# A graph network block on one core: first ffn layer as three-pass split products, convolution bias added by POOL, new step orders

## The chip, the cores and the metric

The kernel runs on one core of one Trainium2 chip. The core has TensorE (PE, matrix products), VectorE (DVE), ScalarE (ACT), GpSimd (POOL) and SyncE (SP, which here issues every DMA). Each engine runs its own list of instructions in order, and the engines wait for each other by semaphores only. The metric is device time in microseconds (us), the median of the runs; one more execution was profiled.

## The reference, cut to what matters

`x` is 16 batches of 512 nodes with 256 features, `adj` one 512 x 512 graph for all of them. Everything is float32. Two layers follow each other, each with a norm and a relu ahead of it and a residual behind it:

```python
h = relu(layernorm(x))
h = elu(gat_heads(h, adj, W_heads, a_heads))     # 4 heads, softmax over 512 neighbours
out = elu(gat_heads(h, adj, W_out[None], a_out)) # one more head ("back"), input width 4 * 256
ffn = relu(out @ w1 + b1) @ w2 + b2
x = x + layernorm(ffn + out) * gamma + beta
h = relu(layernorm(x))                           # second layer, a graph convolution
deg = a.sum(axis=1)                              # a = adj as float
x = x + deg[None, :, None] * (h @ Wi.T + b) + einsum('ij,bjo->bio', a, h @ Wj.T)
```

The change touches `out @ w1` and the term `deg * b`.

## The kernel before

A batch lies as 4 tiles of 128 nodes. The work of a batch is cut into named steps, and every engine has a written list of words `step:which@batch`. `FIRST` and `LAST` are lists of their own for the start and the end (in `LAST` batches are counted from the end, so -1 is the last one), and `ROUND` is run for t = 8 to 15, where `@k` stands for batch t - k. Batches overlap in this way: while the heads of one batch run, the ffn of the one before and the convolution of the one before that are under way. A step has a part on several engines, each under the same name in the list of its engine; nothing reorders the lists at run time.

The steps of one batch, in the order of the data:

- `load`, `norm_in`, `norm_in_out` (statistics on DVE, the power of -0.5 on POOL, scale and relu on ACT), `turn_in` (PE transposes; ACT copies the high part and DVE subtracts it to get the low part).
- `m1:hp`, the product with the weights of head h for half p of the nodes; `f2turn`, `f2send`, `f2bcast`: one column of scores is transposed, sent to HBM and broadcast to all partitions by SP.
- for ten units (five heads, two halves; units 4 and 5 are the back head): `rowmax`, `rowmath` (DVE), `args` (ACT), `rinv`, `scale` (DVE), `turn_p` (8 transposes on PE), `probs` (ACT high part, DVE low part), `attend` (24 matmuls), `elu_neg`, `elu_exp` (ACT), `elu_out` (DVE), `hx` (ACT), `hx_lo` (POOL).
- `mix2` (24 matmuls for each of 4 tiles), then the back head's units.
- `turn_out` (8 transposes of `out` and one ACT copy to `ff[:, 0]`, float32), `ffn1` (float32 products with `w1`, relu on ACT), `ffn2` (float32), `add_b2`, `norm_ff`, `gamma`, `x_beta`, `x2`.
- `norm_gc`, `norm_gc_out`, `turn_gc`, `conv_in:0` and `conv_in:1` (products of both halves of `W_gc`; DVE adds `deg` times the left half to `xb`), `conv` (32 matmuls with the transposed graph), `store`.

Most products are split: both operands are held as an f32r high part and an f32r low part, and `product` sums high x high, low x high and high x low, three matmuls in place of one float32 product. The float32 products are `ffn1`, `ffn2` and all transposes; a float32 product shows as two records in the trace. In `conv_in` the bias enters through a fourth kind of matmul: `pick` has ones in two rows, `brow` holds the bias as a high and a low row, and `also=` places that one matmul of 256 columns behind the first one of each tile, four for each batch.

PSUM is four pairs of banks. Every PE step takes the pair that has been in use longest (`take` waits until it was read, `lend` says by whom), so a step can start only when the step four places ahead of it in PE's list has been read out.

## Time and profile before

| | before |
|---|---|
| median of 3 runs | 1393.72 us (1392.29 to 1399.7) |
| profiled execution, its own time | 1393.09 us |
| span from the first to the last instruction | 1391.3 us |
| mean granted TensorE clock | 0.984 |
| busy share: PE, PE weight load, DVE, ACT, POOL | 95%, 89%, 79%, 80%, 25% |
| DMA, mean | 40 GB/s |

All durations below come from the profiled execution. Its own time is its span plus 1.8 us around it. A busy share counts the time in which at least one instruction of the engine runs. Matmuls are pipelined: a matmul of 256 columns lasts 0.28 us in its record while the next one starts 0.12 us later, so what a matmul takes from the engine is read from the distance of starts, not from the duration.

### The profile page before, as it was taken

The numbers are of one execution on the slowest core, as the hardware profiler recorded it, in microseconds if no ns is written. First come the engines' busy times: TensorE is split into PE (matmuls) and PEld (weight loads), VectorE is DVE, ScalarE is ACT, GpSimd is POOL, SyncE is SP. The second block draws the span as 40 slices with busy tenths as digits, with TensorE's granted clock in tenths as the row PEclk, the third lists the DMA queues.
The fourth block names the chain that finished last, engine by engine and source line by source line (L and its number), as shares of the span: only waits on it lengthen the run. The fifth ranks groups of instructions, "written<-read, shape, count | busy, mean of one in ns | idle before, by whom it ended". The sixth has DMA issues, their size and how long they took to land.

```text
span 1391.3 us, 27533 instructions
## 1 busy us (share of the span) xinstructions
PE 1317.3 (95%) x10024; PEld 1243.7 (89%) x10024; DVE 1101.2 (79%) x2859; ACT 1113.2 (80%) x2143; POOL 341.1 (25%) x234
## 2 busy tenths in 40 slices
PE   3799999999999999999999999999999999999884
PEld 3799999999999999999999999999999989999763
DVE  7798878897888888788888878888787878878442
ACT  4789988888888888888888888888788878878531
POOL 0021222314132131413213141231414132131411
PEclk9799999999999999999999999999999999999997
DMA  6101011011111101111110111110111020011000
GB/s 211 62 24 54 17 32 47 25 38 32 39 46 32 46 24 33 37 39 47 31 47 18 30 46 39 47 31 17 43 43 39 24 61 17 17 39 39 24 31 16
DMA packets 42742, 55.15 MB, mean 40 GB/s; under 512 B 2864, under 2 KB 30832, under 8 KB 42480
## 3 DMA queue, kind: packets, MB, share of 16 engines
q1 hardware_dynamic: 42608, 53.39, 12.6%
q8 instruction: 81, 1.33, 0.4%
q14 instruction: 53, 0.43, 0.1%
HBM read 44.83 MB, written 8.55 MB: 38 GB/s over the span
## 4 chain that ended last, share of the span: by engine, by line
PE 85%; DVE 5%; ACT 4%; DMA 3%; issue 2%; POOL 0%; SPq 0%; POOLq 0%; ACTq 0%
PE ps L1007 60%; PE ps L1077 9%; PE ps L1177 5%; PE ps L1141 4%; PE ps L1129 4%; DMA f_rows<-f2row 2%; PE ps L1150 1%; PE ps L1039 1%; PE ps L1115 1%; DVE arg L898 1%; ACT arg L700 1%; PE ps L1068 1%; PE ps L1010 1%; DVE prob_lo L875 1%; ACT prob_hi L706 0%
## 5 line engine op out<-in xcount | busy, mean ns | idle before, releaser
L598 POOL TENSOR_TENSOR hx_lo<-elu,hx_hi 128x512 fp32r<-128x512 f32 x128 | 168.0, 1314 | 827.6 <-ACT hx_hi L730 827.6
L1007 PE MATMUL ps<-prob_hi,whx_hi 128*128 128x256 f32 x1024 | 297.9, 291 | 3.0 <-DVE prob_lo L875 2.8
L1007 PE MATMUL ps<-prob_hi,whx_lo 128*128 128x256 f32 x1024 | 289.2, 282 | 0.0
L1007 PE MATMUL ps<-prob_lo,whx_hi 128*128 128x256 f32 x1024 | 289.1, 282 | 0.0
L898 DVE CUSTOM_DVE_ANT_0 arg<-f2bc,mask 128x512 f32<-128x512 f32 x320 | 233.6, 767 | 11.8 <-DMA f2bc<-f_rows 10.5
L700 ACT ACTIVATE arg<-arg,nmax 128x512 f32<-128x512 f32 x320 | 227.1, 713 | 1.9 <-DVE nmax L909 1.8
L875 DVE TENSOR_TENSOR prob_lo<-ps,prob_hi 128x1024 fp32r<-128x1024 f32 x160 | 195.1, 1220 | 37.8 <-ACT prob_hi L706 37.2
L696 ACT ACTIVATE arg<-arg,fcol 128x512 f32<-128x512 f32 x320 | 212.4, 714 | 7.5 <-DVE gmax L898 7.5
L1007 PEld LDWEIGHTS ps<-prob_hi,whx_hi 128*128 128x128 f32 x1024 | 195.3, 191 | 6.0 <-DVE prob_lo L875 4.0
L1007 PEld LDWEIGHTS ps<-prob_hi,whx_lo 128*128 128x128 f32 x1024 | 195.7, 191 | 0.6 <-issue 0.5
L1007 PEld LDWEIGHTS ps<-prob_lo,whx_hi 128*128 128x128 f32 x1024 | 195.5, 191 | 0.0
L706 ACT ACTIVATE prob_hi<-ps 128x1024 fp32r<-128x1024 f32 x160 | 162.2, 1015 | 27.9 <-PE ps L1077 27.1
L1077 PE MATMUL ps<-ident,arg 128*128 128x128 f32 x1280 | 167.8, 275 | 7.1 <-DVE arg L924 6.5
L1077 PEld LDWEIGHTS ps<-ident,arg 128*128 128x128 f32 x1280 | 146.2, 142 | 17.7 <-DVE arg L924 7.3
L1007 PE MATMUL ps<-wh_hi,hT_hi 128*128 128x258 f32 x512 | 152.5, 298 | 6.2 <-DVE hT_lo L875 5.8
L1007 PE MATMUL ps<-wo_hi,hx_hi 128*128 128x258 f32 x512 | 146.4, 286 | 0.2 <-POOL hx_lo L598 0.2
L1007 PE MATMUL ps<-wh_lo,hT_hi 128*128 128x258 f32 x512 | 146.2, 286 | 0.0
L924 DVE TENSOR_SCALAR arg<-arg,rinv 128x512 f32<-128x512 f32 x320 | 144.0, 493 | 2.7
L1007 PE MATMUL ps<-wh_hi,hT_lo 128*128 128x258 f32 x512 | 145.7, 285 | 0.0
L1007 PE MATMUL ps<-wo_lo,hx_hi 128*128 128x258 f32 x512 | 144.7, 283 | 0.0
L1007 PE MATMUL ps<-wo_hi,hx_lo 128*128 128x258 f32 x512 | 144.4, 282 | 0.0
L935 DVE SCALAR_TENSOR_TENSOR elu<-elu,ps 128x512 f32<-128x512 f32 x128 | 87.7, 685 | 67.3 <-ACT elu L725 66.0
(131 smaller groups left out, 3144.1 us busy)
## 6 DMA issues: line engine op xcount, KB each, us to landing
f2bc<-f_rows SPq DMA_DIRECT2D x80, 256.0 KB, 3.3
xin<-in_x SPq DMA_DIRECT2D x16, 512.0 KB, 4.1
xb<-in_x SPq DMA_DIRECT2D x16, 512.0 KB, 3.9
out_x<-xb SPq DMA_DIRECT2D x16, 512.0 KB, 2.9
f_rows<-f2row SPq DMA_DIRECT2D x80, 2.0 KB
ff<-in_L_gnn_a_heads SPq DMA_DIRECT2D x1, 1024.0 KB, 7.9
arg<-in_adj SPq DMA_DIRECT2D x1, 1024.0 KB, 10.0
ff<-in_L_gnn_W_out SPq DMA_DIRECT2D x1, 1024.0 KB, 5.6
```

The costliest lines, as they stand in the source:

```text
L598: pool.tensor_tensor(out=hx[1][:, 2 * c.h:2 * c.h + 2, c.u * HN:(c.u + 1) * HN], in0=elu[:, c.buf, :, :], in1=hx[0][:, 2 * c.h:2 * c.h + 2 ...
L696: act.activation(a[:, n, :], a[:, n, :], ACT.Prelu, bias=f1[:, n:n + 1], alpha=SLOPE).then_inc(arg_lin, 1)
L700: i = act.activation(a[:, n, :], a[:, n, :], ACT.Exp, bias=nmax[:, c.abuf, n:n + 1], accum_out=rsum[:, c.abuf, n:n + 1])
L706: act.activation(prob[0][:, c.buf, :, :].rearrange("p j i -> p (j i)"), pairs[c.pair][:, :, :].rearrange("p a n -> p (a n)"), ACT.Copy).th ...
L875: return dve.tensor_tensor(out=dst, in0=src, in1=hi.bitcast(fp32), op=ALU.subtract)
L898: dve.tensor_tensor_reduce(out=arg[:, c.abuf, n, :], in0=f2bc[:, head % F2S, :], in1=mask[:, 2 * c.u + n, :], scale=1.0, scalar=-3.0e38, o ...
L924: i = dve.tensor_scalar(arg[:, c.abuf, n, :], arg[:, c.abuf, n, :], rinv[:, c.abuf, n:n + 1], None, ALU.mult)
L935: dve.scalar_tensor_tensor(out=dst, in0=elu[:, c.buf, :, :], scalar=-1.0, in1=pairs[c.pair][:, :, 0:F], op0=ALU.add, op1=ALU.max).then_inc ...
L1007: i = pe.matmul(out, a, b_, start=(k == 0), stop=(k == n - 1))
L1077: i = pe.transpose(p[:, j, n, :], arg[:, c.abuf, n, j * P:(j + 1) * P], ident[:, :])
L1129: i = pe.matmul(pairs[c.pair][:, o, :], w1_sb[:, k, o * P:(o + 1) * P], outT[:, k, :], start=(k == 0), stop=(k == KC - 1))
L1177: i = pe.matmul(pairs[c.pair][:, n // 2, (n % 2) * F:(n % 2 + 1) * F], adjT[:, j, n * P:(n + 1) * P], mj, start=(j == 0 and s == 0), stop= ...
```

## The change

Three things change.

1. `w1` is held as f32r high and low parts (`w1_prep` on ACT, `w1_low` on DVE, once), `turn_out` gets a high part by ACT and a low part by DVE, both in `h2T` in place of `ff[:, 0]`, and `ffn1` becomes 12 f32r matmuls of 512 columns by `product`. ACT's `turn_out` waits for `conv` of the batch before, since that one reads `h2T`. `w1` is staged in the second slot of `f2bc`, so the first broadcast to that slot waits for `w1_low`.
2. The matmuls with `pick` and `brow` go, and with them what prepared them. Once, DVE computes `deg_b` (degree times bias, 4 instructions, `degb`), and POOL adds it to `xb` in each batch (`bias`), behind `norm_gc_out` and ahead of DVE's accumulation in `conv_in`.
3. All lists of all engines are new. Apart from the new steps (`w1_prep`, `w1_low`, `degb`, `bias`, DVE's `turn_out`) and `brow`, which goes, they hold the same steps in another order.

```diff
@@ -7,239 +7,239 @@
     "SP": """
-    load@0 load@1 load_wo@0 f2send:0@0 f2bcast:0@0 f2send:1@0 load_adj@0 f2bcast:1@0 load@2 f2send:2@0 f2bcast:2@0 f2send:3@0
...
+    load@0 load@1 f2send:0@0 load_wo@0 f2bcast:0@0 f2send:1@0 f2bcast:1@0 f2send:2@0 f2send:3@0 f2bcast:2@0 f2bcast:3@0
...
     "PE": """
-    turn_in@0 gc_turn@0 m1:00@0 m1:01@0 m1:10@0 f2turn:0@0 m1:11@0 f2turn:1@0 m1:20@0 m1:21@0 m1:30@0 m1:31@0 turn_p:0@0
-    f2turn:2@0 adj_turn:0@0 adj_turn:1@0 turn_p:1@0 turn_in@1 attend:0@0 attend:1@0 f2turn:3@0 turn_p:2@0 m1:00@1 turn_p:3@0
...
+    turn_in@0 m1:00@0 m1:01@0 m1:10@0 m1:11@0 f2turn:0@0 gc_turn@0 m1:20@0 m1:21@0 m1:30@0 f2turn:1@0 f2turn:2@0 m1:31@0
+    turn_p:0@0 f2turn:3@0 turn_p:1@0 turn_in@1 attend:0@0 attend:1@0 m1:00@1 turn_p:2@0 turn_p:3@0 attend:2@0 m1:01@1
+    adj_turn:0@0 turn_p:6@0 attend:3@0 f2turn:0@1 m1:10@1 m1:11@1 turn_p:7@0 attend:6@0 adj_turn:1@0 f2turn:1@1 attend:7@0
...
     "ACT": """
-    wh_prep:0@0 wh_prep:1@0 wh_prep:2@0 norm_in_out@0 wh_prep:3@0 mask:0@0 gc_turn@0 turn_in@0 m1:00@0 m1:01@0 mask:1@0
-    m1:10@0 wo_prep:0@0 f2turn:0@0 m1:11@0 m1:20@0 m1:21@0 f2turn:1@0 m1:30@0 norm_in_out@1 m1:31@0 args:0@0 args:1@0
...
+    wh_prep:0@0 wh_prep:1@0 norm_in_out@0 turn_in@0 w1_prep@0 m1:00@0 wh_prep:2@0 wh_prep:3@0 mask:0@0 m1:01@0 m1:10@0 m1:11@0
+    f2turn:0@0 gc_turn@0 m1:20@0 mask:1@0 m1:21@0 m1:30@0 f2turn:1@0 wo_prep:0@0 args:0@0 args:1@0 norm_in_out@1 m1:31@0
...
     "DVE": """
-    norm_in@0 norm_in_out@0 wh_low:0@0 wh_low:1@0 wh_low:2@0 wh_prep:0@0 wh_prep:1@0 wh_prep:2@0 mask:0@0 wh_low:3@0
-    wh_prep:3@0 mask_end:0@0 turn_in@0 mask:1@0 norm_in@1 gc_turn@0 m1:00@0 mask_end:1@0 norm_in_out@1 m1:01@0 m1:10@0
-    wo_prep:0@0 wo_prep:1@0 m1:11@0 wo_prep:2@0 wo_prep:3@0 wo_prep:4@0 wo_prep:5@0 rowmax:0@0 wo_prep:6@0 wo_prep:7@0
-    rowmath:0@0 rowmax:1@0 rowmath:1@0 rinv:0@0 m1:20@0 scale:0@0 m1:21@0 m1:30@0 rowmax:2@0 m1:31@0 rinv:1@0 rowmath:2@0
...
+    norm_in@0 norm_in_out@0 wh_low:0@0 wh_low:1@0 wh_prep:0@0 wh_prep:1@0 turn_in@0 mask:0@0 wh_prep:2@0 wh_low:2@0 m1:00@0
+    wh_prep:3@0 m1:01@0 m1:10@0 wh_low:3@0 mask_end:0@0 m1:11@0 mask:1@0 m1:20@0 gc_turn@0 mask_end:1@0 norm_in@1 rowmax:0@0
+    rowmath:0@0 w1_low@0 m1:21@0 rowmax:1@0 rowmath:1@0 wo_prep:0@0 norm_in_out@1 wo_prep:1@0 rowmax:2@0 rinv:0@0 wo_prep:2@0
+    m1:30@0 scale:0@0 rowmath:2@0 rinv:1@0 wo_prep:3@0 m1:31@0 scale:1@0 probs:0@0 rowmax:3@0 wo_prep:4@0 wo_prep:5@0
...
 ROUND = {
...
     "PE": """
-    m1:31@5 turn_in@4 attend:1@5 f2turn:2@5 turn_p:2@5 m1:00@4 turn_gc@7 m1:01@4 turn_p:3@5 attend:2@5 conv_in:0@7 f2turn:3@5
-    conv_in:1@7 turn_p:4@6 attend:3@5 m1:10@4 turn_p:5@6 attend:4@6 f2turn:0@4 turn_p:6@5 attend:5@6 conv@7 m1:11@4 turn_p:7@5
-    turn_out@6 attend:6@5 ffn1@6 turn_p:8@5 attend:7@5 m1:20@4 turn_p:9@5 f2turn:1@4 attend:8@5 m1:21@4 ffn2@6 m1:30@4
-    attend:9@5 turn_p:0@4 mix2:0@5 mix2:1@5 turn_p:1@4 mix2:2@5 mix2:3@5 attend:0@4 f2turn:-1@5
+    f2turn:2@5 turn_p:2@5 m1:00@4 turn_gc@7 turn_p:3@5 m1:01@4 attend:2@5 conv_in:0@7 f2turn:3@5 conv_in:1@7 turn_p:4@6
+    attend:3@5 m1:10@4 turn_p:5@6 attend:4@6 turn_p:6@5 f2turn:0@4 attend:5@6 m1:11@4 conv@7 turn_out@6 attend:6@5 turn_p:7@5
+    turn_p:8@5 ffn1@6 f2turn:1@4 attend:7@5 attend:8@5 turn_p:9@5 m1:20@4 m1:21@4 ffn2@6 m1:30@4 attend:9@5 mix2:0@5
+    turn_p:0@4 mix2:1@5 turn_p:1@4 mix2:2@5 mix2:3@5 attend:0@4 f2turn:-1@5 m1:31@4 turn_in@3 attend:1@4
...
     "ACT": """
...
+    elu_neg:3@6 elu_exp:3@6 m1:10@5 hx:2@6 probs:5@7 hx:3@6 elu_neg:4@7 elu_exp:4@7 probs:6@6 args:7@6 elu_neg:5@7 elu_exp:5@7
+    f2turn:0@5 m1:11@5 args:8@6 turn_out@7 elu_neg:6@6 elu_exp:6@6 probs:7@6 hx:6@6 probs:8@6 args:9@6 ffn1@7 elu_neg:7@6
...
     "DVE": """
...
+    norm_in@5 elu_out:4@8 probs:6@7 rowmax:8@7 rinv:7@7 rowmath:8@7 elu_out:5@8 m1:11@6 scale:7@7 norm_in_out@5 conv@9
+    rowmax:9@7 rinv:8@7 scale:8@7 turn_out@8 elu_out:6@7 probs:7@7 rowmath:9@7 probs:8@7 rowmax:0@6 rinv:9@7 rowmath:0@6
...
+    norm_ff@8 m1:30@6 elu_out:9@7 rinv:1@6 scale:1@6 norm_ff_out@8 rowmath:2@6 rowmax:3@6 probs:0@6 mix2:0@7 probs:1@6 x2@8
+    rowmath:3@6 rinv:2@6 norm_gc@8 mix2:1@7 scale:2@6 rinv:3@6 norm_gc_out@8 elu_out:0@6 scale:3@6 m1:31@6 turn_in@5
+    elu_out:1@6 probs:2@6 m1:00@5 turn_gc@8 rowmax:4@7
...
     "POOL": """
-    hx_lo:0@5 hx_lo:1@5 hx_lo:2@5 hx_lo:3@5 norm_in@3 hx_lo:6@5 add_b2@6 hx_lo:7@5 hx_lo:8@5 x_beta@6 norm_ff@6 hx_lo:9@5
-    gamma@6 norm_gc@6
+    hx_lo:0@5 bias@7 hx_lo:1@5 hx_lo:2@5 hx_lo:3@5 norm_in@3 hx_lo:6@5 hx_lo:7@5 add_b2@6 hx_lo:8@5 x_beta@6 norm_ff@6
+    hx_lo:9@5 gamma@6 norm_gc@6
...
 LAST = {
...
     "PE": """
...
-    attend:8@-1 turn_p:9@-1 ffn2@-2 attend:9@-1 mix2:0@-1 mix2:1@-1 mix2:2@-1 mix2:3@-1 f2turn:-1@-1 turn_gc@-2 conv_in:0@-2
-    turn_p:4@-1 conv_in:1@-2 turn_p:5@-1 attend:4@-1 attend:5@-1 conv@-2 turn_out@-1 ffn1@-1 ffn2@-1 turn_gc@-1 conv_in:0@-1
-    conv_in:1@-1 conv@-1
...
+    attend:8@-1 attend:9@-1 mix2:0@-1 mix2:1@-1 mix2:2@-1 mix2:3@-1 turn_gc@-2 f2turn:-1@-1 conv_in:0@-2 conv_in:1@-2 conv@-2
+    turn_p:4@-1 turn_p:5@-1 attend:4@-1 attend:5@-1 turn_out@-1 ffn1@-1 ffn2@-1 turn_gc@-1 conv_in:0@-1 conv_in:1@-1 conv@-1
...
@@ -278,18 +278,16 @@
...
-        w1_sb = sb("w1_sb", [P, KC, F])
+        w1x = [sb(f"w1_{s}", [P, KC, F], f32r) for s in ("hi", "lo")]
@@ -330,12 +328,14 @@
...
+        w1_st = f2bc[:, 1, :].rearrange("p (k o) -> p k o", k=KC)
...
+        deg_b = ff[:, 0, :, :]
@@ -343,6 +343,7 @@
...
+        outT = [t[:, :, :].rearrange("p c f -> p (c f)").rearrange("p (k n) -> p k n", k=KC) for t in h2T]
@@ -522,7 +526,7 @@
...
-            sp.dma_start(w1_sb[:, :, :], w1.rearrange("(k p) o -> p k o", p=P)).then_inc(ld[LD_W1], 16)
+            sp.dma_start(w1_st, w1.rearrange("(k p) o -> p k o", p=P)).then_inc(ld[LD_W1], 16)
@@ -546,6 +550,8 @@
...
+                if head == 1:
+                    sp.wait_ge(s_w1, 1)
...
             def load_back(c):
@@ -559,7 +565,6 @@
...
             def load_wo(c):
...
-                sp.wait_ge(s_pick, 1)
@@ -579,14 +584,9 @@
         def _(pool):
...
-            pool.memset(pick_st, 0.0).then_inc(s_zeroed, 1)
-            pool.wait_ge(s_zeroed, 3)
+            pool.wait_ge(s_zeroed, 2)
...
-            for z in range(2):
-                pool.affine_select(out=pick_st, in_=pick_st, compare_op=ALU.not_equal, fill=1.0, base=-z,
-                                   pattern=[[0, P]], channel_multiplier=1).then_inc(s_const, 1)
-                pool.wait_ge(s_const, 2 + z)
@@ -619,7 +619,13 @@
...
+            def bias(c):
+                if c.b == 0:
+                    pool.wait_ge(s_bias, 1)
+                pool.wait_ge(ln_out["gc"], c.b + 1)
+                pool.tensor_tensor(out=xb[:, :, :], in0=xb[:, :, :], in1=deg_b, op=ALU.add).then_inc(bias_added, 1)
@@ -638,6 +644,10 @@
             def wo_prep(c):
...
+            def w1_prep(c):
+                act.wait_ge(ld[LD_W1], 16)
+                act.activation(w1x[0][:, :, :], w1_st, ACT.Copy).then_inc(s_w1_hi, 1)
@@ -730,22 +740,19 @@
...
             def mix2(c):
-                if c.b == 0:
-                    act.wait_ge(s_brow, 1)
...
             def turn_out(c):
+                act.wait_ge(o_turned, c.b + 1)
+                wait(act, conv_done, c.b)
+                act.activation(outT[0], pairs[c.pair][:, :, :], ACT.Copy).then_inc(oT_ready, 1)
...
+            def ffn1(c):
...
-                act.wait_ge(o_turned, c.b + 1)
-                act.activation(ff[:, 0, :, :], pairs[c.pair][:, :, :].rearrange("p a n -> p (a n)").rearrange("p (k n) -> p k n", k=NC),
-                               ACT.Copy).then_inc(oT_ready, 1)
...
-            def ffn1(c):
-                if c.b == 0:
@@ -817,23 +824,23 @@
...
-                if c.info == 0:
-                    dve.wait_ge(s_const, 3)
-                    dve.tensor_copy(pick[:, :], pick_st).then_inc(s_pick, 1)
...
             def gc_turn(c):
...
-            def brow_(c):
+            def w1_low(c):
+                dve.wait_ge(s_w1_hi, 1)
+                dve.tensor_tensor(out=w1x[1][:, :, :], in0=w1_st, in1=w1x[0][:, :, :].bitcast(fp32), op=ALU.subtract).then_inc(s_w1, 1)
...
+            def degb(c):
...
-                part, hi = wk[:, 3, :], w2x[:, 0, :]
-                link(dve.tensor_copy(hi, b_g))
-                link(dve.tensor_tensor(out=part, in0=b_g, in1=hi.bitcast(fp32), op=ALU.subtract))
-                link(dve.tensor_scalar(part, part, ident[:, 1:2], None, ALU.mult))
-                link(dve.scalar_tensor_tensor(out=part, in0=hi.bitcast(fp32), scalar=ident[:, 0:1], in1=part, op0=ALU.mult, op1=ALU.add))
-                dve.tensor_copy(brow[:, :], part).then_inc(s_brow, 1)
+                dve.wait_ge(s_adj, 1)
+                dve.wait_ge(s_adj_turned, 2)
+                for n in range(NC):
+                    i = dve.tensor_scalar(deg_b[:, n, :], b_g, deg[:, n:n + 1], None, ALU.mult)
+                i.then_inc(s_bias, 1)
@@ -928,7 +935,7 @@
...
-                        dve.wait_ge(s_brow, 1)
+                        dve.wait_ge(s_bias, 1)
@@ -940,6 +947,10 @@
...
+            def turn_out(c):
+                dve.wait_ge(oT_ready, c.b + 1)
+                lo(outT[1], pairs[c.pair][:, :, :], outT[0]).then_inc(oT_lo, 1)
@@ -962,7 +973,7 @@
...
-                dve.wait_ge(ln_out["gc"], c.b + 1)
+                dve.wait_ge(bias_added, c.b + 1)
@@ -998,7 +1009,7 @@
...
-            def product(out, terms, also=None):
+            def product(out, terms):
@@ -1006,8 +1017,6 @@
...
-                        if also and k == 1:
-                            pe.matmul(*also, start=False, stop=False)
...
             def gc_turn(c):
@@ -1114,20 +1123,19 @@
...
-                lend((c.pair,), (oT_ready, c.b + 1))
...
-            outT = ff[:, 0, :, :].rearrange("p c f -> p (c f)").rearrange("p (k n) -> p k n", k=KC)
+                lend((c.pair,), (oT_lo, c.b + 1))
...
             def ffn1(c):
...
-                    pe.wait_ge(ld[LD_W1], 16)
-                pe.wait_ge(oT_ready, c.b + 1)
+                    pe.wait_ge(s_w1, 1)
+                pe.wait_ge(oT_lo, c.b + 1)
...
-                    for k in range(KC):
-                        i = pe.matmul(pairs[c.pair][:, o, :], w1_sb[:, k, o * P:(o + 1) * P], outT[:, k, :], start=(k == 0), stop=(k == KC - 1))
-                    i.then_inc(f1_done, 1)
+                    part = slice(o * P, (o + 1) * P)
+                    product(pairs[c.pair][:, o, :],
+                            [(w1x[0][:, k, part], w1x[1][:, k, part], outT[0][:, k, :], outT[1][:, k, :]) for k in range(KC)]).then_inc(f1_done, 1)
...
             def ffn2(c):
@@ -1155,14 +1163,12 @@
             def conv_in_(c):
...
-                    pe.wait_ge(s_brow, 1)
...
-                                [(h2T[0][:, n, k * P:(k + 1) * P], h2T[1][:, n, k * P:(k + 1) * P], wg[0][:, k, :], wg[1][:, k, :]) for k in range(KC)],
-                                also=(pairs[c.pair][:, i, 0:F], pick[:, :], brow[:, :]))
+                                [(h2T[0][:, n, k * P:(k + 1) * P], h2T[1][:, n, k * P:(k + 1) * P], wg[0][:, k, :], wg[1][:, k, :]) for k in range(KC)])
...
```

## Rows read from the trace of the kernel before

**Rows 1.** Page, part 1: busy us, share of span, instructions.

```profile
PE 1317.3 (95%) x10024; PEld 1243.7 (89%) x10024; DVE 1101.2 (79%) x2859; ACT 1113.2 (80%) x2143; POOL 341.1 (25%) x234
```

**Rows 2.** Windows: busy us (instructions) by engine, granted clock, DMA share, GB/s.

```profile
0.00:40.00 40.00, 17.24 (x95) 15.88 (x96) 30.91 (x132) 15.36 (x31) 3.47 (x12) 0.96 0.56 184
...
40.00:80.00 40.00, 29.15 (x212) 27.98 (x211) 32.84 (x98) 34.90 (x75) 2.75 (x2) 0.83 0.22 67
...
400.00:800.00 400.00, 398.08 (x3087) 379.02 (x3086) 335.15 (x844) 336.06 (x647) 106.90 (x70) 1.00 0.12 34
...
1300.00:1340.00 40.00, 33.59 (x238) 31.06 (x238) 20.91 (x56) 19.05 (x36) 7.01 (x5) 0.91 0.02 7
...
1340.00:1391.30 51.30, 25.07 (x117) 19.25 (x116) 13.98 (x33) 8.77 (x14) 9.06 (x5) 0.80 0.10 31
```

**Rows 3.** Groups by line, TensorE: count, busy us, mean ns, idle.

```profile
L1129 PE MATMUL ps<-ff,w_sb 128*128 128x512 f32 x128 | 57.7, 594 | 1.2 <-ACT ff L744 1.1
...
L1010 PE MATMUL ps<-brow,pick 128*128 128x256 f32 x64 | 18.5, 289 | 0.0
```

**Rows 4.** Timeline of TensorE, conv_in of one batch: start, duration, line.

```profile
693.12 0.28 PE L1010 MATMUL ps<-brow,pick 128*128 128x256 f32 x1
...
693.23 0.40 PE L1007 MATMUL ps<-wg_hi,h2T_lo 128*128 128x512 f32 x1
...
694.40 0.39 PE L1007 MATMUL ps<-wg_hi,h2T_hi 128*128 128x512 f32 x1
```

**Rows 5.** Timeline of TensorE: turn_out, ffn1 and what follows.

```profile
718.32 1.04 PE L1115 MATMUL ps<-ident,wk 128*128 128x128 f32 x8
...
722.06 3.59 PE L1129 MATMUL ps<-ff,w_sb 128*128 128x512 f32 x8
...
725.49 1.04 PE L1077 MATMUL ps<-ident,arg 128*128 128x128 f32 x8
...
726.28 0.36 PE L1007 MATMUL ps<-prob_hi,whx_hi 128*128 128x256 f32 x1
...
726.49 0.28 PE L1007 MATMUL ps<-prob_hi,whx_lo 128*128 128x256 f32 x1
```

**Rows 6.** Groups by line of DVE and POOL.

```profile
L875 DVE TENSOR_TENSOR h2T_lo<-ps,h2T_hi 128x1024 fp32r<-128x1024 f32 x16 | 19.6, 1223 | 11.8 <-ACT h2T_hi L758 11.8
...
L834 DVE TENSOR_SCALAR wk<-wk,ident 128x256 f32<-128x256 f32 x1 | 0.4, 353 | 0.0
...
L605 POOL TENSOR_TENSOR wk<-wk,b_bc 128x1024 f32<-128x1024 f32 x16 | 38.4, 2403 | 45.4 <-PE ps L1115 45.4
```

**Rows 7.** Timelines of POOL and DVE: gamma beside a rowmax.

```profile
749.21 2.86 POOL L619 TENSOR_TENSOR wk<-wk,gamma_bc 128x1024 f32<-128x1024 f32 x1 [0.67 <-ACT wk L667]
...
749.75 2.87 DVE L898 CUSTOM_DVE_ANT_0 arg<-f2bc,mask 128x512 f32<-128x512 f32 x1
```

**Rows 8.** Timelines of ACT and DVE: norm_gc_out, conv_in.

```profile
679.90 2.06 ACT L667 ACTIVATE ff<-xb,shift_gc,rstd_gc 128x256 f32<-128x256 f32 x4
...
698.27 0.87 DVE L968 SCALAR_TENSOR_TENSOR xb<-ps,deg,xb 128x256 f32<-128x256 f32 x2
```

**Rows 9.** Timelines of ACT, DVE, TensorE: the first 50 us.

```profile
9.54 2.06 ACT L667 ACTIVATE xin<-xin,shift_in,rstd_in 128x256 f32<-128x256 f32 x4
...
19.50 1.01 ACT L675 ACTIVATE hT_hi<-ps 128x1024 fp32r<-128x1024 f32 x1
...
20.76 1.22 DVE L875 TENSOR_TENSOR hT_lo<-ps,hT_hi 128x1024 fp32r<-128x1024 f32 x1
...
48.50 1.97 PE L1077 MATMUL ps<-ident,arg 128*128 128x128 f32 x8 [6.00 <-DVE arg L924]
```

**Rows 10.** Chain that ended last: the last 80 us.

```profile
1314.35 0.61 ACT w2x_hi L738
...
1321.71 0.68 DVE arg L898
...
1342.03 0.89 PE ps L1115 x8
```

More of the change, by code:

```diff
@@ L67 @@
+    probs:0@1 rowmax:3@1 rinv:2@1 mix2:0@0 scale:2@1 rowmath:3@1 degb@0 rinv:3@1 m1:31@1 norm_in_out@2 scale:3@1 probs:1@1
+    elu_out:0@1 mix2:1@0 probs:2@1 turn_in@2 elu_out:1@1 m1:00@2 rowmax:4@0
     """,
@@ L180 @@
[L180 to L183 removed]
+    f2turn:-1@-7 m1:31@-6 hx:0@-6 turn_in@-5 norm_gc_out@-8 elu_neg:1@-6 elu_exp:1@-6 probs:2@-6 f2turn:2@-6 m1:00@-5
```

368 lines of the change are left out of this document (179 added, 189 removed).

## The prediction

> **What bounds the kernel now.** I read the page first for the busy shares, then the windows, to see where each engine has room, then the groups of TensorE and its timeline for what a matmul takes, and last the waits and the chain at both ends. TensorE is busy 95% of the span, the next engines 80% and 79% [rows 1]. The windows say where the missing 5% lies. From 400 to 800 us TensorE is busy 398.08 of 400 us at full clock, while DVE and ACT are busy 335 and 336 us and POOL 107 [rows 2]. In the first 80 us it is busy 46.4 us (17.24 + 29.15), and in the last 51.3 us only 25.07, there at a mean granted clock of 0.80 [rows 2]. So the kernel has three parts: a start and an end in which chains through several engines decide, and between them some 1220 us in which the time is the sum of what TensorE issues. A microsecond taken from TensorE's list in the middle is worth one microsecond, as long as the others keep up.
>
> **ffn1.** Before, one ffn1 is 8 records of 512 columns, from 722.06 to the next step's start at 725.49: 3.43 us [rows 5]. The new one is 12 f32r matmuls of 512 columns. The same form runs in conv_in: five starts from 693.23 to 694.40, 0.234 us each [rows 4]. 12 x 0.234 = 2.81 us, a gain of 0.62 us for a batch, 9.9 us for 16. One bound is that nothing comes of it in batches where ffn1 then waits for its operand; the other is 10 us.
>
> **The bias matmuls.** There are 64 [rows 3], and the one at 693.12 is followed at 693.23 [rows 4], so one takes 0.11 us; other matmuls of 256 columns are up to 0.12 apart. 64 x 0.115 = 7.4 us (7.0 to 7.7).
>
> **Changes of type.** The first f32r matmul after float32 transposes takes 726.49 - 726.28 = 0.21 us, 0.09 more than its neighbours [rows 5]. Counting such places in TensorE's lists gives 226 before and 229 after, with ffn1 counted on its new side: +0.3 us. Sum for TensorE: 9.9 + 7.4 - 0.3 = 17.0 us less.
>
> **What the others get.** DVE gets 16 subtractions of 1024 columns at 1.22 us [rows 6], 19.6 us, and loses only the single preparation of the bias rows; w1_low (one subtraction of 512 columns, about half of that) and degb (4 x 0.35 us [rows 6]) come once. DVE goes from 79% to about 82%, still below TensorE. ACT's turn_out stays one copy of 1024 columns, 1.01 us as in turn_in [rows 9], and w1_prep comes once. POOL gets 16 additions of 2.40 us [rows 6], 38 us on an engine that is idle for three quarters of the span. The cover of the new low part is the work between turn_out and ffn1. Before, that was one attend, from about 719.1 (718.32 and 0.8 us of transposes) to 722.06, 2.9 us [rows 5]. In the new round it is attend:6, turn_p:7 and turn_p:8, 2.9 + 2 x 0.79 = 4.5 us (one turn_p is 725.49 to 726.28 [rows 5]). Needed are 1.01 + 1.22 = 2.2 us, so some 2.2 us are left for a queue on ACT or DVE. If the cover went, each batch would pay up to these 2.2 us. Behind ACT's turn_out stand elu_neg:6 and probs:7, and attend:7 waits for the latter. Its new wait for conv of the batch before costs nothing: conv stands directly ahead of turn_out in TensorE's list. The bias step starts when norm_gc_out ends, at 681.96 in the batch of [rows 8], and DVE's accumulation comes at 698.27: 16 us for 2.4 us of work. In the last batch turn_gc, its two copies and conv_in (12 x 0.234 x 2 = 5.6 us) lie in between, about 9 us, so it is hidden there too. Behind bias on POOL stand hx_lo:1 to hx_lo:3; a late norm_gc_out would delay them, then elu_neg:3 on ACT, which waits for the buffer. For waits that the new lists bring to the middle I add 2 us. Its idle share is 1.92 of 400 us [rows 2], 0.5%, which is 6 us over 1220: if all of it went, the term would be -6, and if it became three times as much, +12.
>
> **The start.** Before, ACT's turn_in runs at 19.50, 8 us after norm_in_out ended at 11.60, because the mask step and gc_turn stand ahead of it, and the first product waits for its low part until 21.98 [rows 9]. In the new lists nothing but the transposes (2.0 us at the low clock, as for those at 48.50 [rows 9]) stands between: 11.6 + 2.0 + 1.0 + 1.2 = 15.8, some 6 us earlier. w1_prep is put ahead of ACT's m1:00, where it must wait for the load of w1; m1:00 on TensorE runs meanwhile. Next late is the first turn_p, at 48.50 for want of scale:0. On DVE three wo_prep steps stand ahead of scale:0 in place of eight, but f2bcast:0 now stands behind load_wo on SP, whose wait for the prepared weights and whose 1 MB come first, and f2bcast:1 waits for w1_low. adj_turn, at the low clock before, moves behind the first attends. DVE is busy 30.9 of the first 40 us [rows 2], so I do not take the whole 6 us: 4 us gained, between 8 gained and 3 lost.
>
> **The end.** From the last mix2 (1314.35) to turn_out of the last batch (1342.03) the chain takes 27.7 us [rows 10]; the conv of the batch before, 32 matmuls of 256 columns x 0.12 = 3.8 us, stands in it directly ahead of turn_out. In the new list this conv stands ahead of turn_p:4, in the time in which the last softmax is on its way (its rowmax starts 7.4 us after mix2 [rows 10]). Against these 3.8 us go the low part of turn_out, 1.2 us, and that ACT's args:4 and DVE's rowmath:4 now stand behind conv_in:1, about 1 us. I take 1.5 us gained, between 4 gained and 3 lost.
>
> **The sum.** -17.0 - 4 - 1.5 + 2 = -20.5 us. On the profiled execution's 1393.09 us that is 1372.6. The median of the runs lies 0.6 us above that execution, so 1373.
>
> **The shared port.** A POOL step can hold DVE up: the rowmax that starts at 749.75, 0.54 us into POOL's gamma, takes 2.87 us and ends with it [rows 7], where another takes 0.68 [rows 10]. The Trainium skill, SBUF — State Buffer, section Who interferes with whom, says that a DVE instruction with two SBUF inputs, or a tensor_scalar in a two-port mode, and a GpSimd instruction that reads SBUF exclude each other, and the later one is blocked for the whole instruction; by that rule the trace agrees. By the same rule the bias step would lock out a rowmax or a scale sixteen more times, and if each met one and all of it reached TensorE, the sum would be 15 us longer than before instead of 20 shorter.
>
> **Rivals.**
>
> *The middle gives back part.* The lists are rigid, and a late copy or a buffer still in use in each batch costs TensorE half a microsecond: 16 x 0.5 = 8 us on top of the sum, 1381. For it: DVE gets 19.6 us, and ACT and DVE are at 84% of the middle [rows 2]. Against: the margin of 2.2 us at the one new chain. Chance 0.2.
>
> *The ends lose.* load_wo ahead of the broadcast delays the first softmax, and the last one is delayed by conv_in:1: no gain at the end and 1 us lost at the start, 5.5 + 1 us on top, 1379.5. Chance 0.1.
>
> *Slower: bias blocks DVE.* Each bias locks out one rowmax or scale for up to 2.87 - 0.68 = 2.2 us, and what hangs on it is late on TensorE: 16 x 2.2 = 35 us on top, 1408. It decides (0.5% slower) from (20.5 + 7) / 16 = 1.7 us for a batch. For it: [rows 7]. Against: in the new round DVE runs elu_out:1, probs:2, m1:00 and turn_gc while bias is due, each with an operand in PSUM, and rowmax:4 only behind them; and DVE has 16% of the middle to catch up. Chance 0.05.
>
> *Nothing comes of it.* TensorE's busy share only hides that another chain sets the pace, and its shorter work turns into waiting: 1392. Against: 398 of 400 us busy, and starts that follow each other at the pipeline's distance. Chance 0.05.
>
> **How the numbers follow.** My forecast has 0.6, with 1366 to 1379 as its own range. The range goes down to 1365, a little below start and end both at their good bounds (1373 - 4 - 2.5 = 1366.5), and up through the first two rivals to 1385, where the middle's term is at its bound of +12. That leaves out the last two rivals and some margin, 2 in 10. A measurement here tells about 0.5%, 7 us, from no change. Faster by that: the forecast and the first two rivals, 0.9; within it: the fourth, 0.05; slower: the third, 0.05.
>
> **What would show it.** ffn1 as 12 starts 0.23 us apart and no L1010 group; TensorE still busy above 99% from 400 to 800 us, with a distance between equal steps of successive batches about 1.1 us shorter; ffn1 without idle time ahead of it; DVE's added group of 16 at 1.22 us; first product near 16 us and first turn_p before 48.5; DVE's rowmax and scale no longer on average. The prediction is wrong if TensorE's idle time in the middle comes to more than 18 us, or if the start or the end moves by more than its bounds.

## The result, and the profile of the changed kernel

The changed kernel takes 1377.67 us, the median of 4 runs (1376.74 to 1378.36); the kernel before has 1396.71 in 4 runs (1392.29 to 1400.56). The ratio is 0.9876, with a 95% interval of 0.9849 to 0.9903: 1.2% faster. 1373 was forecast with a range of 1365 to 1385. The profiled executions differ by 14.7 us (1393.09 and 1378.36; spans 1391.3 and 1376.6), where the sum forecast 20.5. That is 4 us less than the medians tell, because all runs of the kernel before lie in two groups, 1391.1 to 1394.4 and 1396.1 to 1400.6 us, and the profiled one is of the faster group; what sets the two apart is not shown.

The page, part 1, answers to [rows 1].

```profile
span 1376.6 us, 27572 instructions
...
PE 1299.2 (94%) x10024; PEld 1248.1 (91%) x10024; DVE 1100.5 (80%) x2874; ACT 1113.1 (81%) x2144; POOL 370.1 (27%) x247
```

TensorE is busy 18.1 us less and idle 77.4 us instead of 74.0: -18.1 + 3.4 = -14.7. The windows, columns as in [rows 2], say where the idle time is.

```profile
0.00:80.00 80.00, 48.41 (x318) 45.20 (x319) 66.23 (x237) 52.95 (x108) 5.32 (x11) 0.87 0.40 129
80.00:160.00 80.00, 74.58 (x612) 72.28 (x611) 64.02 (x173) 71.94 (x143) 15.39 (x12) 1.00 0.11 28
240.00:1200.00 960.00, 959.86 (x7545) 929.23 (x7544) 808.82 (x2068) 827.72 (x1594) 278.55 (x181) 1.00 0.12 38
1200.00:1290.00 90.00, 84.45 (x645) 80.36 (x644) 63.57 (x159) 67.89 (x129) 31.03 (x20) 1.00 0.08 22
```

The same windows of the kernel before:

```profile
0.00:80.00 80.00, 46.39 (x304) 43.87 (x305) 63.75 (x229) 50.26 (x105) 6.22 (x14) 0.89 0.39 125
80.00:160.00 80.00, 77.58 (x624) 73.73 (x623) 69.25 (x181) 74.18 (x145) 18.03 (x13) 1.00 0.11 31
240.00:1200.00 960.00, 955.51 (x7385) 907.26 (x7384) 796.27 (x2020) 812.52 (x1563) 252.46 (x166) 1.00 0.12 36
1200.00:1290.00 90.00, 89.13 (x676) 82.94 (x675) 70.09 (x173) 74.33 (x142) 20.18 (x13) 1.00 0.12 39
```

At the start the new kernel gets 2.0 us ahead in the first 80 us and gives 3.0 back in the next 80. In the middle its idle time falls from 4.49 us of 960 to 0.14. From 1200 to 1290 us TensorE is idle 5.55 us where it was idle 0.87. The new kernel is 20 us ahead there; over the same work of the kernel before, from 1220 to 1311.6 us, the idle time is 0.87 us as well.

A clean measure of the middle is the distance between POOL's gamma steps of successive batches (timeline of POOL; start, duration): first before, then after.

```profile
505.07 2.86 POOL L619 TENSOR_TENSOR wk<-wk,gamma_bc 128x1024 f32<-128x1024 f32 x1 [0.68 <-ACT wk L667]
586.41 2.86 POOL L619 TENSOR_TENSOR wk<-wk,gamma_bc 128x1024 f32<-128x1024 f32 x1 [0.67 <-ACT wk L667]
```

```profile
501.11 2.41 POOL L619 TENSOR_TENSOR wk<-wk,gamma_bc 128x1024 f32<-128x1024 f32 x1 [0.62 <-ACT wk L677]
580.50 2.41 POOL L619 TENSOR_TENSOR wk<-wk,gamma_bc 128x1024 f32<-128x1024 f32 x1 [0.63 <-ACT wk L677]
```

A batch takes 79.39 us instead of 81.34, 1.95 less. Forecast were 1.1. Gamma itself is 0.45 us shorter; in [rows 7] it ran beside a rowmax, and here no rowmax starts while it runs.

ffn1 is now three groups of 64 matmuls (TensorE's groups; busy us, mean ns, idle before), to be held against L1129 in [rows 3]. No group is left for brow and pick.

```profile
L1018 PE MATMUL ps<-h2T_hi,w_hi 128*128 128x512 f32 x64 | 27.3, 427 | 2.4 <-DVE h2T_lo L882 2.4
L1018 PE MATMUL ps<-h2T_hi,w_lo 128*128 128x512 f32 x64 | 26.4, 413 | 0.0
L1018 PE MATMUL ps<-h2T_lo,w_hi 128*128 128x512 f32 x64 | 26.1, 408 | 0.0
```

ffn1 waits 2.4 us in all, and that is the last batch alone. In the middle it waits for nothing (outT's parts lie in the h2T buffers and bear their name), but by little. Timelines of TensorE, ACT and DVE around one ffn1:

```profile
706.14 1.03 PE L1124 MATMUL ps<-ident,wk 128*128 128x128 f32 x8
706.93 0.36 PE L1018 MATMUL ps<-prob_hi,whx_hi 128*128 128x256 f32 x1
...
711.55 0.48 PE L1018 MATMUL ps<-h2T_hi,w_hi 128*128 128x512 f32 x1
```

```profile
707.21 1.03 ACT L751 ACTIVATE h2T_hi<-ps 128x1024 fp32r<-128x1024 f32 x1 [0.65 <-PE ps L1124]
```

```profile
708.89 0.89 DVE L931 TENSOR_SCALAR arg<-arg,rinv 128x512 f32<-128x512 f32 x2
709.69 1.22 DVE L882 TENSOR_TENSOR h2T_lo<-ps,h2T_hi 128x1024 fp32r<-128x1024 f32 x1
```

The high part is there at 708.24, but DVE still has rowmax:9, rinv:8 and scale:8 ahead of the low part, which starts at 709.69 and is ready at 710.91. Counted from the attend at 706.93, it takes 3.98 us, and the cover is 4.62. The margin is 0.64 us.

The end, timeline of TensorE (in square brackets the idle time before, and what ended it):

```profile
1323.23 1.97 PE L1124 MATMUL ps<-ident,wk 128*128 128x128 f32 x8 [2.07 <-DVE wk L942]
1327.58 0.80 PE L1018 MATMUL ps<-h2T_hi,w_hi 128*128 128x512 f32 x1 [2.37 <-DVE h2T_lo L882]
...
1328.60 0.63 PE L1018 MATMUL ps<-h2T_lo,w_hi 128*128 128x512 f32 x1
1329.02 0.63 PE L1018 MATMUL ps<-h2T_hi,w_hi 128*128 128x512 f32 x1
```

turn_out takes 1.97 us where it took about 1.04, and ffn1's matmuls start 0.42 us apart and not 0.23. The granted clock is 0.53 from 1323.23 to 1333.84, nearly all of it at the lower of the two levels (1.2 GHz); before the change it was 1.00 over the same steps (1342.03 to 1347.70).

### The profile page after: what moved, and what is told of

It reads as the page before. It is cut to its first block, busy times and chain, and to the rows that moved or that the text cites. A ratio compares the mean times of both kernels' runs of the same rounds, so it can differ in the third digit from the quotient of the medians.

```text
span 1376.6 us, 27572 instructions
## 1 busy us (share of the span) xinstructions
PE 1299.2 (94%) x10024; PEld 1248.1 (91%) x10024; DVE 1100.5 (80%) x2874; ACT 1113.1 (81%) x2144; POOL 370.1 (27%) x247
## 4 chain that ended last, share of the span: by engine, by line
PE 86%; ACT 5%; DVE 5%; issue 2%; DMA 1%; POOL 0%; SPq 0%; ACTq 0%; DVEq 0%
PE ps L1018 66%; PE ps L1086 9%; PE ps L1183 4%; PE ps L1149 4%; PE ps L1124 1%; PE ps L1158 1%; PE ps L1048 1%; ACT arg L710 1%; DVE arg L905 1%; DVE prob_lo L882 1%; ACT prob_hi L716 1%; PE ps L1077 1%; ACT arg L706 1%; ACT elu L731 1%; DMA f2bc<-f_rows 0%
## 5 line engine op out<-in xcount | busy, mean ns | idle before, releaser
L905 DVE CUSTOM_DVE_ANT_0 arg<-f2bc,mask 128x512 f32<-128x512 f32 x320 | 220.9, 728 | 4.3 <-PE ps L1086 2.9
L931 DVE TENSOR_SCALAR arg<-arg,rinv 128x512 f32<-128x512 f32 x320 | 147.0, 502 | 1.4
L731 ACT ACTIVATE elu<-ps 128x512 f32<-128x512 f32 x160 | 93.9, 587 | 64.6 <-PE ps L1018 62.2
```

What stands on the lines that cost most here:

```text
L731: act.activation(elu[:, c.buf, :, :], pairs[c.pair][:, :, 0:F], ACT.Relu, scale=-1.0).then_inc(elu_neg, 1)
L905: dve.tensor_tensor_reduce(out=arg[:, c.abuf, n, :], in0=f2bc[:, head % F2S, :], in1=mask[:, 2 * c.u + n, :], scale=1.0, scalar=-3.0e38, o ...
L931: i = dve.tensor_scalar(arg[:, c.abuf, n, :], arg[:, c.abuf, n, :], rinv[:, c.abuf, n:n + 1], None, ALU.mult)
```

## The experiments

Ratios are to runs of the kernel before on the same chip. The experiments ran on three chips, whose kernels before have medians of 1397.35 (e1 to e4), 1396.55 (e5 to e8) and 1394.03 us (e9 to e12), so medians of different groups can differ by up to 3 us for that alone. A batch is the mean of two distances between gamma steps, from about 430 to 590 us, and does not hang on this.

| run | median us | ratio to before, 95% interval | a batch, us |
|---|---|---|---|
| before | 1396.7 | 1 | 81.34 |
| changed kernel | 1377.67 | 0.9876 (0.9849 to 0.9903) | 79.40 |
| e1 both changes, old orders | 1412.79 | 1.0111 (1.0088 to 1.0133) | 81.8 |
| e2 new orders alone | 1392.56 | 0.9972 (0.9958 to 0.9986) | 80.50 |
| e3 ffn1 alone, old orders | 1415.57 | 1.0134 (1.0113 to 1.0156) | 82.0 |
| e4 bias alone, old orders | 1394.19 | 0.9982 (0.9965 to 0.9999) | 80.8 |
| e5 e1, ffn1 behind attend:7 | 1442.68 | 1.0344 (1.0321 to 1.0366) | 82.7 |
| e6 changed, conv behind attend:5 | 1379.84 | 0.9887 (0.9869 to 0.9905) | 79.4 |
| e7 changed, m1:21 first | 1375.17 | 0.9851 (0.9829 to 0.9873) | 79.4 |
| e8 changed, bias twice | 1388.62 | 0.9948 (0.9930 to 0.9966) | 80.10 |
| e9 e5, low part behind probs:7 | 1448.32 | 1.0383 (1.0358 to 1.0407) | 82.2 |
| e10 ffn1 alone, new orders | 1384.15 | 0.9929 (0.9908 to 0.9951) | 79.86 |
| e11 bias alone, new orders | 1386.14 | 0.9937 (0.9917 to 0.9958) | 80.05 |
| e12 e7 and a new last batch | 1389.13 | 0.9961 (0.9946 to 0.9976) | 79.4 |

**e1.** The new code in the lists of before, with the new steps put in.

```diff
 DVE ROUND
-    ... probs:7@5 ...
+    ... turn_out@6 probs:7@5 ...
 POOL ROUND
-    ... hx_lo:0@5 hx_lo:1@5 ...
+    ... hx_lo:0@5 bias@7 hx_lo:1@5 ...
 PE ROUND (as before)
     turn_p:7@5 turn_out@6 attend:6@5 ffn1@6 turn_p:8@5 attend:7@5
```

> Both code changes (first layer in three f32r passes, bias on POOL), but the steps of every engine in the orders of the kernel before; the new steps are put in by hand: DVE's turn_out ahead of probs:7, POOL's bias behind hx_lo:0 of two batches on, the preparations of the start behind m1. Theory A (the gain is TensorE's work, the orders only make room for it): the middle keeps nearly all of the 17 us of removed work, less about 1 us for each turn_out that has only attend:6 behind it; the start stays that of before, the end too. Median about 1382, 1379 to 1387. Rival B (the code alone gains nothing, the new orders are what makes it faster): 1391 to 1397, with ffn1 waiting for oT_lo over 1 us in each batch. Rival C (the new orders cost more at the start and the end than they give in the middle): under 1377.

1.1% slower than before, outside the range of all three; B's sign is there, a wait of ffn1 of over 1 us. TensorE's timeline and its group of ffn1 name the place:

```profile
644.80 1.04 PE L1126 MATMUL ps<-ident,wk 128*128 128x128 f32 x8
649.78 0.50 PE L1020 MATMUL ps<-h2T_hi,w_hi 128*128 128x512 f32 x1 [1.09 <-DVE h2T_lo L884]
```

```profile
L1020 PE MATMUL ps<-h2T_hi,w_hi 128*128 128x512 f32 x64 | 28.0, 438 | 23.0 <-DVE h2T_lo L884 22.8 <-DVE prob_lo L884 0.2
```

With attend:6 alone as cover, ffn1 waits for the low part in every batch, 22.8 us in all, more than the 17 us of removed work. The chain takes as long as in the changed kernel: the low part is ready at 649.73, 4.1 us behind the attend at 645.59. Here the queue is on ACT, though: its high part starts only at 647.25, behind args. TensorE is busy 8.7 us less than before and idle 25.5 us more (1308.6 of a span of 1408.1), so ffn1's waits are nearly all of the added idle time. That the busy time falls by 8.7 and not by 17 is in part the clock (mean granted 0.979, before 0.984) and the start of each wait, which counts as busy (see e2); the rest is open.

**e2.** The code of before in the new lists.

```diff
 DVE FIRST
-    ... probs:1@0 ...
+    ... probs:1@0 brow@0 ...
 (no turn_out, w1_prep, w1_low, degb, bias; all else as in the change)
```

> The code of the kernel before (fp32 first layer, bias as a matmul) in the new orders of every engine, with the steps that this code lacks left out and brow behind probs:1 of the first batch on DVE. Theory A (orders make room, work makes the gain): within 4 us of the kernel before, 1391 to 1400; the period of a batch stays between 80.5 and 81.5 us. Rival B (orders are the gain): 1378 to 1386. Rival C (the orders lose at both ends): 1400 to 1408, with the loss in the last four batches.

Faster by 0.3%. The median is what A expects, the batch is not: it is 0.84 us shorter, 1.0%, without any change of the work. Some 0.45% of it is idle time (4.49 us of the 960 from 240 to 1200 us before, 0.12 in e2). The rest counts as busy, but most of it is waiting too. TensorE's timeline of the kernel before, ahead of turn_gc and ahead of conv:

```profile
523.51 0.28 PE L1007 MATMUL ps<-wh_lo,hT_hi 128*128 128x258 f32 x1
524.00 1.06 PE L1150 MATMUL ps<-ident,ff 128*128 128x128 f32 x8 [0.21 <-DVE elu L935]
...
548.91 0.28 PE L1007 MATMUL ps<-w2x_lo,prob_hi 128*128 128x256 f32 x1
549.30 0.36 PE L1177 MATMUL ps<-h2T_hi,adjT 128*128 128x256 f32 x1
```

turn_gc starts 0.49 us behind the matmul ahead of it, in e2 0.16; conv 0.39, in e2 0.12. Together that is 0.6 of the 0.84 us. Only 0.3 of it shows as idle time, because the record of a matmul lasts 0.28 us where the next could start after 0.12: the first 0.16 us of a wait lie under it. So the old orders had two short waits in each batch, and the new ones have none. At the ends it is lost again: the profiled span is 1391.6 us, 0.3 more than before; of the gain only the 0.3% between the medians is left.

**e3 and e4.** One code change each in the old lists.

```diff
 e3: product(pairs[c.pair][:, i, :], [...],
+        also=(pairs[c.pair][:, i, 0:F], h2T[0][:, n, 0:P], wg[0][:, 0, 0:F]))
 e4: ffn1
+    i = pe.matmul(pairs[c.pair][:, o, :], w1x[0][:, k, part].bitcast(fp32), outT[0][:, k, :].bitcast(fp32), ...)
```

> The first layer in three f32r passes alone, in the orders of before. The bias stays on TensorE as a matmul of the same shape as before, but its operands are other tiles at hand (a piece of h2T and a row of wg), so the bias added is not that of the reference; POOL adds none. By the prediction's terms the work falls by 9.9 us and rises by 0.3: median 1384 to 1390 if the terms add up in the old orders, with 12 records in a group of ffn1 0.234 us apart. Rival (ffn1 waits for DVE's low part, which comes 2.2 us after turn_out while attend:6 covers 2.0): each batch gives back 0.3 us or more, 1389 to 1394.

> The bias on POOL alone, in the orders of before; the first layer stays at fp32 rate with four matmuls (it reads the rounded high parts only, so its result lacks the low parts; their number, shape and type of pass are those of before). By the prediction's terms 64 matmuls of 0.116 us go, 7.4 us: median 1385 to 1390. Rival (POOL's addition blocks the port it shares with DVE for about 2 us a batch and DVE is late for it): 1392 to 1400, with rowmax means over 780 ns.

e3 is 1.3% slower, worse than its rival, which had priced the missing cover at 0.2 us; its three-pass ffn1 waits just as in e1. e4 gains 0.5 us a batch, as the 0.46 of its matmuls, but its median is 0.2% under before, not 0.5%, and lies in the range of its rival. The rival's sign came too, a mean of 789 ns for rowmax (767 before), but not its cause in the middle: from 500 to 600 us the only long rowmax are those beside gamma, 2.88 us as before. What takes the gain back outside the middle is open. So what makes e1 slow in the middle is ffn1's operand alone.

**e5 and e9.** Both try to mend e1 by moving steps.

```diff
 e5, PE ROUND
-    turn_out@6 attend:6@5 ffn1@6 turn_p:8@5 attend:7@5
+    turn_out@6 attend:6@5 turn_p:8@5 attend:7@5 ffn1@6
 e9, also DVE ROUND
-    turn_out@6 probs:7@5
+    probs:7@5 turn_out@6
```

> Experiment e1 with one step moved: in TensorE's lists ffn1 stands behind attend:7 instead of behind attend:6, so that turn_p:8 and attend:7 (4 us) run while ACT and DVE make the high and low part of outT; ACT's and DVE's lists are those of e1. Theory A2 (e1 lost only by the wait of ffn1 for oT_lo, 1.7 us in each of 16 batches): about 27 us less than e1 less what the first batch loses because ffn2 stands directly behind: 1385 to 1392, no wait for h2T_lo over 0.5 us in the middle, period 80.2 to 80.8 us. Rival D (DVE's and ACT's queues in the old orders are what is late, whichever step shows it): the waits come back in front of other steps, median over 1400.

> Experiment e5 with one more step moved: DVE makes the low part of outT behind probs:7 instead of ahead of it, so that attend:7, which e5 put ahead of ffn1, no longer waits for it. Theory A3 (what the old orders lose is where DVE's new step of 1.2 us stands against probs:7 and ffn1, nothing else): the wait of 1.3 us in front of attend:7 goes, ffn1 starts 6 us behind turn_out with its operand ready, and the period falls from e5's 82.7 us to between 80.2 and 81.3 us; median 1388 to 1402. Rival D (ACT's list, which reads ffn1 where it stood before, delays elu:7 and what follows it): the period stays over 82 us, 1420 to 1440.

Both are far worse than e1. Rival D has e5 and the batch of e9, whose median is still 8 us over D's range. In e5 the wait moves, at first to attend:7:

```profile
663.15 0.35 PE L1020 MATMUL ps<-prob_hi,whx_hi 128*128 128x256 f32 x1 [1.26 <-DVE prob_lo L884]
```

because its prob_lo stands behind turn_out's low part. e9 cuts that wait to 0.83 us, but ACT's list still has ffn1's readout where it stood. ACT's timeline in e9:

```profile
666.39 0.69 ACT L761 ACTIVATE ff<-ps,b1c 128x512 f32<-128x512 f32 x1 [0.72 <-PE ps L1020]
667.79 0.69 ACT L761 ACTIVATE ff<-ps,b1c 128x512 f32<-128x512 f32 x1 [0.71 <-PE ps L1020]
668.38 0.59 ACT L733 ACTIVATE elu<-ps 128x512 f32<-128x512 f32 x1
```

ACT now stands still for ffn1 31 times, 55.9 us in all (52.0 in e5, 10.9 in e1), with the elu of head 7 queued behind. That points to the readers' lists, which would have to be changed with TensorE's. A version with ACT's list moved too was not tried, so ACT's share in the loss is read from waits, not isolated. The longer batches make up 14 and 7 us of the 30 and 36 us that e5 and e9 lose to e1; the rest is lost at the start and the end.

**e10 and e11.** The code changes of e3 and e4, one at a time, in the new lists.

> The new orders of e2 with the first layer in three f32r passes alone. The bias stays on TensorE as a matmul of the same shape on other operands at hand (a piece of h2T, a row of wg), so the bias added is not that of the reference; POOL adds none. Theory A (with 4.5 us of other work between turn_out and ffn1 the low part, ready 3.9 us behind turn_out, costs nothing): period 80.50 - 0.62 + 0.02 = 79.9 us, median 1392.6 - 9.6 = 1383, 1381 to 1385. Rival (the low part takes some of it back): 1386 to 1393.

> The new orders of e2 with the bias on POOL alone; the first layer stays at fp32 rate (on the rounded high parts only, so its result lacks the low parts). Theory A (the addition on POOL is covered): period 80.50 - 0.46 = 80.04 us, median 1392.6 - 7.4 = 1385, 1383 to 1387. Rival (it pushes POOL's hx_lo against DVE's rowmax, as the doubled addition of e8 did for 0.7 us a batch): 1387 to 1396.

Theory A has both: 1384.15 and 1386.14 where 1383 and 1385 were expected. By the batch, the split is clean: from e2's 80.50 us, ffn1 takes 0.64, the bias 0.45, both together 1.10. The mean rowmax is 726 ns in e11, so the bias holds none up. POOL's gamma steps in e10, then e11:

```profile
502.20 2.40 POOL L617 TENSOR_TENSOR wk<-wk,gamma_bc 128x1024 f32<-128x1024 f32 x1 [0.62 <-ACT wk L669]
582.07 2.42 POOL L617 TENSOR_TENSOR wk<-wk,gamma_bc 128x1024 f32<-128x1024 f32 x1 [0.60 <-ACT wk L669]
```

```profile
424.35 2.42 POOL L619 TENSOR_TENSOR wk<-wk,gamma_bc 128x1024 f32<-128x1024 f32 x1 [0.60 <-ACT wk L677]
504.38 2.42 POOL L619 TENSOR_TENSOR wk<-wk,gamma_bc 128x1024 f32<-128x1024 f32 x1 [0.60 <-ACT wk L677]
```

**e8.** The bias in two halves.

```diff
-  i = dve.tensor_scalar(deg_b[:, n, :], b_g, deg[:, n:n + 1], None, ALU.mult)
+  i = dve.tensor_scalar(deg_b[:, n, :], b_g, deg[:, n:n + 1], 0.5, ALU.mult, ALU.mult)
+  pool.tensor_tensor(out=xb[:, :, :], in0=xb[:, :, :], in1=deg_b, op=ALU.add).then_inc(bias_half, 1)
+  pool.wait_ge(bias_half, c.b + 1)
   pool.tensor_tensor(out=xb[:, :, :], in0=xb[:, :, :], in1=deg_b, op=ALU.add).then_inc(bias_added, 1)
```

> The changed kernel with the bias added on POOL in two halves, each an addition of the same size (128x1024), one behind the other; the result is the same. It doubles the suspected cost of the port that DVE and POOL share. Theory A (the addition lies beside other work): within 2 us of the changed kernel, POOL busy grows by 16 times 2.4 us, rowmax mean by up to 10 ns. Rival (each addition blocks DVE for its length and TensorE waits for that): 16 times 2.4, 1395 to 1416; from 0.3 us a batch on it would show as over 1382.

11 us slower than the changed kernel, 0.70 a batch. Theory A is wrong for a second addition, and the rival's range is not reached either. POOL, then DVE:

```profile
440.38 2.41 POOL L630 TENSOR_TENSOR xb<-xb,ff 128x1024 f32<-128x1024 f32 x1
442.74 1.30 POOL L600 TENSOR_TENSOR hx_lo<-elu,hx_hi 128x512 fp32r<-128x512 f32 x1
```

```profile
441.20 0.68 DVE L886 TENSOR_TENSOR whx_lo<-ps,whx_hi 128x512 fp32r<-128x512 f32 x1
...
443.14 1.45 DVE L909 CUSTOM_DVE_ANT_0 arg<-f2bc,mask 128x512 f32<-128x512 f32 x1
```

The addition itself blocks nothing: DVE's whx_lo, with an operand in PSUM, takes its usual 0.68 us beside it. But it pushes POOL's hx_lo from in front of rowmax:4 onto it. That rowmax ends 0.55 us behind hx_lo, at 444.59, and takes 1.45 us instead of 0.68; TensorE's conv_in:1 comes 0.4 us late in the batch, and the attend behind it 0.7. In the changed kernel bias ends at 438.52, hx_lo at 440.15, and the rowmax starts at 441.37 and takes 0.68.

**e6.** The conv of the 15th batch back in its old place.

```diff
 PE LAST
-    conv@-2 turn_p:4@-1 turn_p:5@-1 attend:4@-1 attend:5@-1 turn_out@-1
+    turn_p:4@-1 turn_p:5@-1 attend:4@-1 attend:5@-1 conv@-2 turn_out@-1
 DVE LAST
-    conv@-2 probs:5@-1 elu_out:4@-1 elu_out:5@-1
+    probs:5@-1 elu_out:4@-1 elu_out:5@-1 conv@-2
```

> The changed kernel with one step back in its old place: conv of the 15th batch runs directly ahead of the last turn_out (behind attend:5) on TensorE, its readout behind elu_out:5 on DVE. Theory A (moving it forward shortened the chain by 3.8 us but left TensorE waiting before turn_out, so that turn_out and ffn1 of the last batch ran at a granted clock of 0.5): turn_out 1.0 us instead of 2.0, the matmuls of ffn1 0.23 us apart instead of 0.43, which gives 3.3 us back, and the chain grows by up to 3.8: 1376 to 1379, no difference beyond 1.5 us. Rival (the clock at the end does not depend on conv): 1381 to 1383.

The median is 2.2 us over that of the changed kernel, a little over the upper edge of A, but the runs overlap (1378.10 to 1381.69 and 1376.74 to 1378.36, on different chips), so the difference is not clear of noise. The clock did what A says:

```profile
1326.47 1.04 PE L1126 MATMUL ps<-ident,wk 128*128 128x128 f32 x8
1329.88 0.50 PE L1020 MATMUL ps<-h2T_hi,w_hi 128*128 128x512 f32 x1 [2.37 <-DVE h2T_lo L884]
...
1330.45 0.40 PE L1020 MATMUL ps<-h2T_lo,w_hi 128*128 128x512 f32 x1
1330.68 0.39 PE L1020 MATMUL ps<-h2T_hi,w_hi 128*128 128x512 f32 x1
```

turn_out at 1.04 us, ffn1's matmuls 0.23 apart, granted clock 1.00. It starts 3.24 us later, though. The faster clock gives all of that back: ffn2 starts at 1333.72, and in the changed kernel at 1333.84. The 2 us that e6 then loses have another cause. DVE's readout of ffn2, changed kernel first, then e6, and POOL's x_beta of e6:

```profile
1337.60 1.22 DVE L958 TENSOR_TENSOR wk<-ps,wk 128x1024 f32<-128x1024 f32 x1 [10.08 <-PE ps L1149]
```

```profile
1339.62 1.22 DVE L960 TENSOR_TENSOR wk<-ps,wk 128x1024 f32<-128x1024 f32 x1 [9.79 <-POOL wk L607]
```

```profile
1334.86 2.35 POOL L614 TENSOR_TENSOR xb<-xb,beta_bc 128x1024 f32<-128x1024 f32 x1 [38.02 <-DMA xb<-in_x]
```

The readout waits for POOL's add_b2, which stands behind x_beta, and x_beta for the load of `xb`, which can only start when the batch before is stored, and that one ends with conv. In the changed kernel x_beta starts at 1323.38. So what the move of conv brings at the end is that `xb` comes free earlier; the shorter chain to turn_out is paid for in full by the low clock.

**e7.** One readout earlier in DVE's list of the start.

```diff
 DVE FIRST
-    mask_end:1@0 norm_in@1 rowmax:0@0 rowmath:0@0 w1_low@0 m1:21@0
+    mask_end:1@0 m1:21@0 norm_in@1 rowmax:0@0 rowmath:0@0 w1_low@0
```

> The changed kernel with one step moved in DVE's list of the start: the readout m1:21 of the first batch stands ahead of norm_in of the second, rowmax:0, rowmath:0 and w1_low, for which it waited. Theory A (the start is bound by DVE's list: TensorE waits 6.7 us for fcol in front of f2turn:2): the wait shrinks to under 2 us and the time falls by 2 to 5 us, 1372.5 to 1376. Rival (the next transfer or DVE step is as late: rowmax:0 waits for the f2 row, TensorE for turn_p:0): the wait moves to another step, 1376 to 1380.

2.5 us faster than the changed kernel (1373.62 to 1375.85 against 1376.74 to 1378.36, on different chips; the intervals of the two ratios overlap), the lowest median of all versions. TensorE's waits in the start, changed kernel first, then e7:

```profile
36.77 0.38 PE L1077 MATMUL ps<-ident,fcol 128*4 128x128 f32 x1 [6.70 <-DVE fcol L893]
45.55 1.97 PE L1086 MATMUL ps<-ident,arg 128*128 128x128 f32 x8 [5.71 <-DVE arg L931]
```

```profile
31.30 0.27 PE L1078 MATMUL ps<-ident,fcol 128*4 128x128 f32 x1 [1.24 <-DVE fcol L894]
44.53 1.97 PE L1087 MATMUL ps<-ident,arg 128*128 128x128 f32 x8 [11.37 <-DVE arg L932]
```

The wait of 6.7 us shrinks to 1.2, and the next one, for the first scaled softmax, grows from 5.7 to 11.4. Of 5.5 us, 1.0 reaches the first turn_p. Both theories have a part; DVE's chain to scale:0 is what bounds the start up to there. Only 0.5 us is left of it later: the gamma steps of the 15th batch start at 1285.45 and 1285.97. The other 2.0 us of the profiled difference come behind it, where no step was moved: from turn_out to the end the granted clock is 0.73 and not 0.66. So e7 shows no more than 0.5 us for its move, and the rest is the clock, for a reason that is not shown.

**e12.** e7, and the steps ahead of the last mix2 moved.

```diff
 PE LAST
-    turn_out@-2 attend:6@-1 ffn1@-2 attend:7@-1 turn_p:8@-1 ffn2@-2 turn_p:9@-1 attend:8@-1
+    attend:6@-1 turn_out@-2 attend:7@-1 turn_p:8@-1 ffn1@-2 turn_p:9@-1 attend:8@-1 ffn2@-2
 (ACT: ffn1@-2 behind elu_exp:7@-1; DVE: probs:9@-1 ahead of ffn2@-2)
```

> The changed kernel with e7's move at the start and, before the last batch's mix2, five steps of the hand-written order moved: TensorE does attend:6 ahead of turn_out of the 15th batch, attend:7 and turn_p:8 ahead of its ffn1 and attend:8 ahead of its ffn2; ACT's readout of ffn1 stands behind elu_exp:7, DVE's probs:9 ahead of the readout of ffn2. Theory A (the new end loses 2.2 us in front of turn_out and 1.3 us in front of attend:9 because of the order alone): 1370 to 1374. Rival (ffn2 of the 15th batch is then 3 us later, and its norm and turn_gc behind mix2 are the next to be late): 1375 to 1379.

14 us slower than e7, worse than the rival. TensorE's waits:

```profile
1270.60 0.48 PE L1019 MATMUL ps<-prob_hi,whx_hi 128*128 128x256 f32 x1 [3.50 <-DVE prob_lo L883]
...
1283.06 0.35 PE L1019 MATMUL ps<-prob_hi,whx_hi 128*128 128x256 f32 x1 [3.28 <-DVE elu L943]
...
1297.11 0.39 PE L1019 MATMUL ps<-wo_hi,hx_hi 128*128 128x258 f32 x1 [3.11 <-POOL hx_lo L599]
```

The changed kernel's waits of 2.2 us in front of turn_out and 1.3 in front of attend:9 went; three of over 3 us came, for steps of DVE and POOL that the moves made late. So the waits there are not a matter of these steps' order alone, and which order would be better stays open.

## Why the prediction was right, point by point

**TensorE's work, -17.0 forecast: right.** On the new orders the code is worth 1.10 us a batch, 17.6 for 16, split 0.64 and 0.45 where 0.62 and 0.46 were forecast (e10, e11). Over the whole kernel the code brings 15.0 us (spans of e2 and the changed kernel; 14.9 by the medians), so 2.6 of the 17.6 are lost at the ends. DVE, forecast at 82%, stays at 80%: 19.6 us were added, and rowmax takes 12.7 us less.

**ffn1's cover: right in sign, mis-sized.** The prediction had 2.2 us needed of 4.5 us of cover and 2.2 left. It added two durations and no queue: 3.98 us are needed, because DVE has 1.45 us of other steps ahead of the low part and ACT starts 0.28 us late. 0.64 us are left. In the old orders, with one attend as cover, ffn1 waits in each batch and the change as a whole loses 1.1% (e1). The orders are not decoration. The prediction called the new list a cover but not how near it came to the edge.

**Waits of the new lists, +2 forecast: the term that failed, with the other sign.** The new orders by themselves shorten a batch by 0.84 us (e2), 13.4 us if all 16 had it. The prediction took TensorE's idle time as all that there was to gain (6 us over the middle) and so was bounded at half: the page counts the first 0.16 us of each wait as busy, and two waits in each batch, ahead of turn_gc and of conv, make up most of the gain. Why DVE was late for them in the old orders is not shown. One cause may be that rowmax no longer meets gamma: the one long rowmax of a batch takes 1.78 us instead of 2.88, gamma 2.41 instead of 2.86, and the mean of 320 rowmax falls from 767 to 728 ns (727 in e2). No run isolated that.

**The start, -4 forecast: +1.** The first product came at 15.52 us (15.8 forecast) and the first turn_p at 45.55 (before 48.50), and TensorE had 2.0 us more done by 80 us, but 3.0 less from 80 to 160. The prediction looked at the first softmax and not at the batch behind it. e7 shows DVE's list as the bound up to the first turn_p.

**The end, -1.5 forecast: a loss.** From the last mix2 to turn_out the distance shrank as forecast: ACT copies the last part of mix2 at 1297.15 and turn_out starts at 1323.23, 26.1 us, 1.6 less than in [rows 10]. But two things were missed. One is the low clock behind it: from turn_out to the end it is 53.4 us where it was 49.3, at a mean granted clock of 0.66 instead of 0.79. From the last mix2 on, the end is thus 2.5 us longer, still within the bound of 3 lost. The other is 4.7 us more idle time from 1200 to 1290, in the batch before, where the prediction did not look.

**Rivals.** *The middle gives back*, *nothing comes of it*: no; idle 0.14 us of 960. *The ends lose*: yes, by more than its 1 us, hidden by the middle's unforeseen gain. *Bias blocks DVE*: not by the addition, which lies beside steps with an operand in PSUM as forecast. e8 shows the mechanism one step further: 2.4 us more on POOL and the hx_lo behind it meets a rowmax, for 0.70 us a batch. The prediction's row had the locked-out rowmax end with gamma; it ends 0.55 us behind, as the one in e8 does: it is held until POOL is done and then still has most of its own 0.68 us to do.

The sum came near by luck, because two errors cancelled. At 1.95 us a batch, 16 batches would have given 31.2 us, where the forecast had 15.0 (17.0 less 2); but 16.5 of them are missing at the start and in the last batches, where the forecast had a gain of 5.5. Of the 16.5, some 1 us of idle time at the start, 4.7 in the batch before the last and 2.5 behind the last mix2 are seen; the rest is not located. The prediction allowed a loss of 3 us at the start and 3 at the end, 6 together. Measured by the steps that it named, both stay within; measured as all that the first and last batches lose, they do not.

## What to carry to other kernels

When a step gets a second producer in its chain, measure the chain with the queues in front of each producer, not the sum of the durations: here 4.0 us instead of 2.2, and 0.6 us of margin between 1.2% faster and 1.1% slower. In hand-written orders a step has one place in each engine's list; moving it in TensorE's list but not in ACT's (e5, e9) cost more than the wait it was to remove, and even a move in three lists did (e12). Here a wait shorter than 0.16 us does not show as idle time; compare the starts of neighbours with those of a version that does not wait. Read an engine's gain in the middle by the distance between equal steps of successive batches: here it told ffn1's part from the bias's to a few hundredths of a microsecond (e10, e11), and it showed a gain of the orders that the median hid (e2). Before a small difference is put down to an edit, look where in the two traces it arises: of e7's 2.5 us, 2.0 arise where nothing was moved.

## What the hardware showed that was not expected

A POOL addition of 2.4 us leaves DVE steps with a PSUM operand at their length (0.68 us beside it), while a rowmax that starts 0.4 us into a POOL hx_lo of 1.30 us, both working in SBUF, takes 1.45 us (e8). Held up is not only DVE: gamma takes 2.86 us where a rowmax is under way when it starts, and 2.41 without. The Trainium skill, SBUF — State Buffer, section Who interferes with whom, has just the pair in which both read SBUF exclude each other, for the whole instruction; by that rule the trace agrees. The granted clock at the end depended on whether TensorE was fed through the last softmax: 0.53 with 2 us idle ahead of turn_out and again ahead of ffn1, 1.00 with conv in between, which made 1.97 us of turn_out's 1.04 and 0.42 us of the 0.23 between ffn1's matmuls. In e6 this was worth 3.4 us up to the start of ffn2, about as much as the conv that filled the wait had cost.
